# Gates' exponentials moved into the attention layers, silu's table loaded ahead of the tanh, and first chunks ahead of the routing

## What is computed

```python
x = x + _L0_attn_ref(_L0_cond_ref(x, side, side, w, u, cond), ...)
x = x + _L0_ffn_ref(_L0_cond2_ref(x, side, side, w, u, cond), ...)
...
# a gate: two scans over time (forward and back) of exp(k) and exp(k) * v, and then
euk = jnp.exp(jnp.minimum(u + kf, 30.0))
num = nf + nb - ekv + euk * vf
den = df + db - ek + euk
base = jax.nn.sigmoid(r) * (num / jnp.maximum(den, 1e-08))
...
# L0's feed-forward part: 16 experts, of which 6 are taken, and a shared one
scores = jax.nn.softmax(x @ gate_w.T, axis=-1)
topk_w, topk_ids = lax.top_k(scores, TOP_K)
y = jax.nn.silu(g) * u @ w2_.T
```

## Time and profile before

| | us |
|---|---|
| median of the three timed runs | 1056.41 |
| lowest, highest | 1053.12, 1060.1 |
| the profiled execution | 1053.54 |
| its span | 1051.7 |
| busy: TensorE, VectorE, ScalarE, GpSimd | 917.2, 787.1, 522.7, 248.9 |
| mean granted clock of TensorE, of full speed | 0.961 |

### The profile page before, as it was taken

One profiled execution on the slowest core, in us unless ns is written; L12 is line 12 of the kernel. 1 busy time (PEld: TensorE's weight loads), 2 busy tenths in 40 slices (PEclk: granted clock), 3 DMA queues, 4 the chain that ended last, 5 costly groups with the idle time before them and its releaser, 6 DMA issues.

```text
span 1051.7 us, 14774 instructions
## 1 busy us (share of the span) xinstructions
PE 917.2 (87%) x5524; PEld 672.9 (64%) x5524; DVE 787.1 (75%) x1188; ACT 522.7 (50%) x781; POOL 248.9 (24%) x288
## 2 busy tenths in 40 slices
PE   2899898899999998799888989996768886899998
PEld 1566666677777886556555868862445664778886
DVE  7898893459999895867967689887759998554444
ACT  6354446345545554355466444435857666243332
POOL 5122213023334241000020022301623224012221
PEclk9999998899999999879989999997999999899999
DMA  6000000243434330000000243324010000033331
GB/s 248 1 2 2 1 2 1 100 141 87 146 113 145 119 114 31 1 1 1 1 1 1 71 119 117 91 77 104 1 60 1 1 1 4 29 112 111 114 106 60
DMA packets 28518, 64.07 MB, mean 61 GB/s; under 512 B 10240, under 2 KB 12032, under 8 KB 27680
## 3 DMA queue, kind: packets, MB, share of 16 engines
q1 hardware_dynamic: 28448, 63.14, 18.9%
HBM read 60.37 MB, written 2.76 MB: 60 GB/s over the span
## 4 chain that ended last, share of the span: by engine, by line
PE 57%; DVE 22%; ACT 11%; issue 7%; POOL 1%; DMA 1%; DVEq 0%; SPq 0%; ACTq 0%; POOLq 0%
PE bank L1723 10%; PE bank L1724 10%; PE bank L1725 10%; PE bank L639 4%; PE bank L665 3%; DVE act_lo L2073 2%; ACT probs L786 2%; DVE wkv_y L192 2%; DVE bank L2068 2%; PE bank L748 1%; DVE bank L2059 1%; PE bank L2294 1%; DVE wkv_y L269 1%; PE bank L697 1%; DVE act_s L912 1%
## 5 line engine op out<-in xcount | busy, mean ns | idle before, releaser
L1723 PE MATMUL bank<-h_hi,w_gu_hi 128*128 128x512 f32 x416 | 168.1, 404 | 14.3 <-DVE act_lo L2073 11.1
L1870 ACT ACTIVATE act_s<-bank 128x512 f32<-128x512 f32 x104 | 61.8, 597 | 219.1 <-PE bank L1725 219.1
L1725 PE MATMUL bank<-h_lo,w_gu_hi 128*128 128x512 f32 x416 | 165.8, 399 | 0.0
L1724 PE MATMUL bank<-h_hi,w_gu_lo 128*128 128x512 f32 x416 | 165.7, 398 | 0.0
L2059 DVE TENSOR_TENSOR bank<-bank,c_rows 128x512 f32<-128x512 f32 x94 | 65.1, 692 | 87.9 <-PE bank L1725 87.9
L1990 POOL TENSOR_TENSOR w_d_lo<-w_raw,w_d_hi 128x256 fp32r<-128x256 f32 x52 | 46.9, 901 | 268.6 <-ACT w_d_hi L1864 268.6
L1723 PEld LDWEIGHTS bank<-h_hi,w_gu_hi 128*128 128x128 f32 x416 | 79.2, 190 | 41.3 <-issue 20.0
L786 ACT ACTIVATE probs<-bank 128x1536 f32<-128x1536 f32 (+1 forms) x32 | 53.0, 1657 | 99.0 <-PE bank L697 90.6
L1725 PEld LDWEIGHTS bank<-h_lo,w_gu_hi 128*128 128x128 f32 x416 | 78.9, 190 | 19.3
L1985 POOL TENSOR_TENSOR w_gu_lo<-w_raw,w_gu_hi 128x512 fp32r<-128x512 f32 x52 | 71.5, 1374 | 83.2 <-ACT w_gu_hi L1859 83.2
L1724 PEld LDWEIGHTS bank<-h_hi,w_gu_lo 128*128 128x128 f32 x416 | 79.2, 190 | 17.4
(11 more groups left out here) (345 smaller groups left out, 1808.9 us busy)
## 6 DMA issues: line engine op xcount, KB each, us to landing
w_raw<-in_L_w SPq DMA_DIRECT2D x52, 384.0 KB, 3.2
c_rows<-c_L SPq DMA_DIRECT2D x26, 512.0 KB, 3.6
c_rows<-c_L SPq DMA_DIRECT2D x6, 448.0 KB, 3.6
w_attn<-in_L_w_attn SPq DMA_DIRECT2D x2, 1280.0 KB, 7.5
c_rows<-c_L SPq DMA_DIRECT2D x6, 384.0 KB, 3.5
c_rows<-c_L SPq DMA_DIRECT2D x6, 320.0 KB, 3.6
c_rows<-c_L SPq DMA_DIRECT2D x6, 256.0 KB, 3.8
lora_chunks<-w_raw SPq DMA_DIRECT2D x4, 384.0 KB, 2.6
```

Of the source, the lines that this page charges most:

```text
L1723: pe.matmul(o, w_hi, r_hi, start=start, stop=False)
L1724: pe.matmul(o, w_lo, r_hi, start=False, stop=False)
L1725: return pe.matmul(o, w_hi, r_lo, start=False, stop=stop)
L1870: act.activation(act_s[:, half, :], bank[2 * half][:, :], ACT.Silu).then_inc(self.silu, 1)
```

## The change

It does four things.
- The exponentials of gates 2 and 3 (16) leave `Experts.act` of L0 for the last batch of L0's attention, in four groups of four (`gate_exps_act`); the 8 of gate 6 leave L1's experts for the end of L1's attention.
- Ahead of the first tanh of L0's and L1's experts the set of tables with silu is loaded by an own instruction.
- In L0, gate and up of chunk 1 for the first half stand ahead of the logits of the second half, the silu, product and split of chunk 0 for the first half stand in the attention's end, and the routing's exponential stands behind the high parts of the chunks. In L1 the silu and the product of the first half go ahead of the routing. `made` gives the new count of the steps of chunks 0 and 1 in L0.
- Steps of the routing that don't need the one ahead of them no longer wait for it (`note`), and in L3 some are exchanged.

```diff
+        def gate_exps_act(act, n, batches):
+
+            for b in batches:
+                for ch in range(KC):
+                    last = side_exp_act(act, G[:, G_SLOT[n], ch, b * T:b * T + T], ch, n, b)
+            if batches[-1] == B - 1:
+                last.then_inc(wkv_exp, B)
...
@@ -1041,14 +1049,23 @@
                     if b:
                         self.ctx_act(act, b - 1, 1)
                     self.exp_act(act, b, 0)
+                    if b == B - 1:
+                        gate_exps_act(act, 2, (0, 1))
                     if b == 0:
                         act.wait_ge(n_gated, self.first + 1)
                     self.inv_act(act, b, 0)
                     self.exp_act(act, b, 1)
+                    if b == B - 1:
+                        gate_exps_act(act, 2, (2, 3))
                     self.exp_act(act, b, 2)
+                    if b == B - 1:
+                        act.wait_ge(n_gated, B)
+                        gate_exps_act(act, 3, (0, 1))
                     self.scale_act(act, b, 1, 0)
                     self.scale_act(act, b, 1, 1)
                     self.ctx_act(act, b, 0)
+                    if b == B - 1:
+                        gate_exps_act(act, 3, (2, 3))
                     self.units_exp_act(act, b, 1)
                     self.inv_act(act, b, 1)
                 self.exp_act(act, B - 1, 3)
...
@@ -1110,6 +1127,8 @@
                 self.inv_dve(dve, B - 1)
                 self.norm_dve(dve, B - 1, 0)
                 self.norm_dve(dve, B - 1, 1)
+                F0.mul_dve(dve, 0, 0)
+                F0.lo_dve(dve, 0, 0)
                 self.tail_dve(dve, B - 1)
...
                 self.ctx_act(act, B - 1, 1)
+                act.wait_ge(n_proj, 4 * (self.first + B))
+                act.wait_ge(n_vproj, self.first + B)
+                gate_exps_act(act, 6, range(B))
                 F1.tanh_act(act, 0)
...
+            def made(self, p, half):
+
+                return 2 * half + p + 1 if self.plain and p < 2 else self.count(p, half)
...
                 if p:
-                    pe.wait_ge(L.silu if p == 2 and not L.plain else L.mul, L.count(p - 1, half))
+                    pe.wait_ge(L.silu if p == 2 and not L.plain else L.mul, L.made(p - 1, half))
                 else:
...
                 if L.name != "L0":
                     L.logits_pe(pe, 0)
                 if L.name == "L0":
+                    L.gate_up_pe(pe, 1, 0)
                     L.logits_pe(pe, 1)
                 else:
                     L.gate_up_pe(pe, 0, 0)
                     L.logits_pe(pe, 1)
                 L.gate_up_pe(pe, 0, 1)
                 if L.plain:
-                    L.gate_up_pe(pe, 1, 0)
                     L.down_pe(pe, 0, 0)
                     L.gate_up_pe(pe, 1, 1)
                     L.down_pe(pe, 0, 1)
...
             def silu_act(self, act, p, half):
-                act.wait_ge(self.gate_mm, self.count(p, half))
+                act.wait_ge(self.gate_mm, self.made(p, half))
                 if p:
-                    act.wait_ge(self.mul, self.count(p - 1, half))
+                    act.wait_ge(self.mul, self.made(p - 1, half))
                 act.activation(act_s[:, half, :], bank[2 * half][:, :], ACT.Silu).then_inc(self.silu, 1)
...
                 if half == 0:
+                    if L.name != "L3":
+                        act.preload_act_table_set("silu_and_others")
                     act.wait_ge(L.x_ready, L.x_value - B // 2)
                     if L.name == "L0":
                         act.wait_ge(n_tab, 11)
...
-                for unit in L.units[::B]:
-
-                    g = UNITS[unit][0]
-                    if g == 3:
-                        act.wait_ge(n_gated, B)
-                    if g == 6:
-                        act.wait_ge(n_gated, 2 * B)
-                    for b in range(B):
-                        for ch in range(KC):
-                            last = side_exp_act(act, G[:, G_SLOT[g], ch, b * T:b * T + T], ch, g, b)
-                    last.then_inc(wkv_exp, B)
+                if L.plain:
+                    L.silu_act(act, 0, 0)
+                    L.hi_act(act, 0, 0)
                 L.tanh_act(act, 1)
+                if L.name == "L1":
+                    L.silu_act(act, 0, 0)
                 L.split_h_act(act, 1)
-                L.route_act(act)
-                L.silu_act(act, 0, 0)
+                if L.plain:
+                    L.silu_act(act, 1, 0)
+                else:
+                    L.route_act(act)
+                    if L.name == "L3":
+                        L.silu_act(act, 0, 0)
                 L.silu_act(act, 0, 1)
...
                 else:
-                    L.hi_act(act, 0, 0)
-                    L.silu_act(act, 1, 0)
                     L.split_gu_act(act, 2)
                     L.hi_act(act, 0, 1)
+                    L.hi_act(act, 1, 0)
+                    L.route_act(act)
                     L.silu_act(act, 1, 1)
-                    L.hi_act(act, 1, 0)
                     L.copies_act(act)
...
+                if L.name != "L3":
+                    L.mul_dve(dve, 1 if L.plain else 0, 0)
                 L.route0_dve(dve)
-                L.mul_dve(dve, 0, 0)
-                L.route1_dve(dve)
-                L.mul_dve(dve, 0, 1)
                 if L.plain:
-                    L.lo_dve(dve, 0, 0)
-                    L.mul_dve(dve, 1, 0)
+                    L.mul_dve(dve, 0, 1)
                     L.lo_dve(dve, 0, 1)
+                    L.lo_dve(dve, 1, 0)
+                    L.route1_dve(dve)
                     L.mul_dve(dve, 1, 1)
-                    L.lo_dve(dve, 1, 0)
                 else:
+                    L.mul_dve(dve, 0, 0 if L.name == "L3" else 1)
+                    L.route1_dve(dve)
+                    if L.name == "L3":
+                        L.mul_dve(dve, 0, 1)
                     L.route2_dve(dve)
...
-            def done(self, dve, ins):
+            def note(self, ins):
+
                 self.steps += 1
                 ins.then_inc(self.r_step, 1)
+
+            def done(self, dve, ins):
+
+                self.note(ins)
                 dve.wait_ge(self.r_step, self.steps)
...
-                    do(dve.tensor_tensor(tb(3), lg, L.kth(0), ALU.subtract))
-                    do(dve.tensor_tensor(tb(2), lg, L.kth(5), ALU.is_gt))
+                    L.note(dve.tensor_tensor(tb(3), lg, L.kth(0), ALU.subtract))
+                    L.note(dve.tensor_tensor(tb(2), lg, L.kth(5), ALU.is_gt))
                     do(dve.tensor_tensor(tb(4), lg, L.kth(5), ALU.is_equal))
-                    do(dve.tensor_reduce(route_s[:, 0, :], tb(2), AX.X, ALU.add))
+                    L.note(dve.tensor_reduce(route_s[:, 0, :], tb(2), AX.X, ALU.add))
...
                     do(dve.tensor_scalar(tb(2), tb(2), 0.5, 0.5, ALU.mult, ALU.add))
+                    L.note(dve.tensor_scalar(tb(4), tb(2), -1.0, center, ALU.mult, ALU.add))
                     do(dve.tensor_scalar(tb(3), tb(2), lower, None, ALU.is_ge))
+                    L.note(dve.scalar_tensor_tensor(out=tb(4), in0=tb(2), scalar=center, in1=tb(4), op0=ALU.subtract, op1=ALU.max))
                     do(dve.scalar_tensor_tensor(out=tb(3), in0=tb(2), scalar=0.5, in1=tb(3), op0=ALU.is_le, op1=ALU.mult))
-                    do(dve.tensor_scalar(tb(4), tb(2), -1.0, center, ALU.mult, ALU.add))
-                    do(dve.scalar_tensor_tensor(out=tb(4), in0=tb(2), scalar=center, in1=tb(4), op0=ALU.subtract, op1=ALU.max))
                     dve.wait_ge(L.r_act, 2)
...
+                    L.note(dve.tensor_tensor(tb(4), tb(4), tb(3), ALU.mult))
                     L.largest_dve(dve, tb(5))
+                    L.note(dve.tensor_reduce(route_s[:, 0, :], tb(4), AX.X, ALU.add))
```

More of the change, by code:

```diff
@@ L1739, in up_pe @@
                 if p:
-                    pe.wait_ge(L.mul, L.count(p - 1, half))
+                    pe.wait_ge(L.mul, L.made(p - 1, half))
                 if p > (0 if L.plain else 1):
@@ L1873, in hi_act @@
                 if p or self.plain:
-                    act.wait_ge(self.mul, self.count(p, half))
+                    act.wait_ge(self.mul, self.made(p, half))
                 else:
@@ L2055, in weigh_dve @@
                 if p:
-                    dve.wait_ge(L.up_mm, L.count(p, half))
+                    dve.wait_ge(L.up_mm, L.made(p, half))
                 else:
-                    dve.wait_ge(L.mul, L.count(p, half))
+                    dve.wait_ge(L.mul, L.made(p, half))
                 dve.tensor_tensor(m, m, weights, ALU.mult).then_inc(L.weighted, 1)
@@ L2063, in mul_dve @@
                 if p == 0 or p < L.plain:
-                    dve.wait_ge(L.up_mm, L.count(p, half))
+                    dve.wait_ge(L.up_mm, L.made(p, half))
                 else:
                     dve.wait_ge(L.weighted, L.weights(p, half))
-                dve.wait_ge(L.silu, L.count(p, half))
+                dve.wait_ge(L.silu, L.made(p, half))
```

18 lines of the change are left out of this document (8 added, 10 removed).

## The result

The median of 20 runs is 1050.21 us (1047.56 to 1057.36) against 1056.76 us (1050.76 to 1069.41) of 20 runs of the kernel before; the ratio is 0.9946 with a 95% interval from 0.9924 to 0.9969. The forecast was 1050.5.

The account below looks back on a forecast made before the run. TensorE was taken as the bound, busy 917.2 of 1051.7 us, so only its waits and 1.2 GHz stretches could be won. Terms +1.0 − 5.4 + 0.0 − 0.2 = −4.6 from 1055.0 gave 1050.5 us, range 1045.5 to 1057.

Parts of the forecast that it names:

- Part 1: Last batch of L0's attention: sixteen exponentials moved in cost +1.0 us (0.6 by the first group, 0.4 by the fourth).
- a sign of being wrong: The forecast is wrong if L0's last attention batch is over 2 us longer, or its entry distance over 20.
- Part 2: L0's entry: chunk 1 ahead of the logits gains 5.4 us, chunk 2 starting at 205.3 instead of 210.68; bounds −5.6 to −3.3.
- I take 2.4 GHz throughout: L0's entry: TensorE keeps its full clock despite the small gaps, as between 573 and 578.
- the clock stays low: Rival, L0's entry: small gaps add up and the 1.2 GHz stretch stays; gain only 3.3 us, time 1052.5; chance 0.15.
- Those of 0.75 and 0.35: L0's entry: TensorE waits 0.75 us for product (0,1), then 0.35 for the routing's second part before turning the weights.
- Part 3: L1's entry: eight exponentials ahead of the first tanh, 4 us in ScalarE's wait, change 0; bounds −0.4 to +0.4.
- ends this piece: L1's entry: the weights' DMA, for which VectorE waits 4.00 us at 610.67, is issued at about the same time.
- Part 4: L3's entry: two routing waits fewer before the exponential, 0.1 each, gain 0.2 us; bounds −0.6 and 0.
- The dearer table switch: Rival, L0's entry: table loads cost more than their 1.28 us rows, gain 1.4 us less, time 1051.8; chance 0.10.
- The stall of 8 us: Rival, L0's attention: every exponential group delays TensorE, up to +8.0 us, making it 2.4 slower, 1057.4; chance 0.10.
- hidden: Rival, each entry: unmoved transfers or weights set its end; added 1.0 us, gain up to 1, time 1055.0; chance 0.07.

Follow-up runs that it names:

- exps_only: Kernel before with only the exponentials moved (L0's sixteen into its attention's last batch, L1's eight ahead of its first tanh); median 1062.17 us beside 1062.46 of before.
- after_again: The changed kernel run again with no edit, for a second profile; median 1052.28 us beside 1062.46 of the kernel before, ratio 0.9915.
- notes_late: Changed kernel with every routing wait back and, in L0, the split of chunk 2's gate and up weights moved behind silu (1,1); median 1053.81 us.
- two_loads: Changed kernel with two more activation table loads between the routing's exponential and silu (1,1) of L0; median 1054.5 us.
- notes_undone: Changed kernel with a wait behind every routing operation again; median 1052.92 us.
- l0_only: Kernel before with only L0's new order; exponentials, routing waits, L1 and L3 as before; median 1050.48 us beside 1058.29 of before, ratio 0.9926.
- split8_l3: Changed kernel with eight of L0's sixteen exponentials back in its experts, and L3's entry ordered like L1's; median 1050.73 us.

## Why the prediction was right, and where it was not

**Part 1, forecast +1.0.** +0.89 (B of exps_only, after_again and notes_late): 0.60 at the wait of 158.54 and 0.3 at the last score exponential, by the two steps named. What the step left out is the clock: of the seven traces with all groups four have 1.2 GHz in this batch, at 1.6 to 3.3 us. In all four the batch is over 2 us longer than before, which the prediction had named as a sign of being wrong: it took the sum of the waits for the batch's length and had no term for the clock there.

**Part 2, forecast −5.4.** In D −5.1 to −5.3. But in seven of the eleven traces with the new entry C is 16.0 instead of 15.0, although only 3.4 us of it are at 1.2 GHz and not 6.8. Before, the 1.2 GHz lies where TensorE has waits (at full clock it is busy 2.58 of 5.60 us there, 172.1 to 177.7 of after_again); the 3.4 us come behind that, on matmuls without a gap (busy 3.40 of 3.40). C and D together are 40.7 before, 36.2 to 36.7 in ten of the eleven, and 35.6 in the first trace of the changed kernel: some −4.2, and −5.1 in that one. The step that failed is "I take 2.4 GHz throughout". In eight of eleven traces with the new order 3.4 us of D run at 1.2 GHz; the rival "the clock stays low" was half right, with 1.2 of its 2.1 us (the terms written beside it give 2.0). The gaps of 0.45 and 0.6 came as 0.53 and 0.46. Those of 0.75 and 0.35 vanished where TensorE ran slow, and were 0.39 and 0.10 where it didn't (two_loads), so that the distance at full clock is an estimated 17.6 us instead of 17.9.

**Part 3, forecast 0.** F1 is 0.69 shorter, outside the bound of −0.4: the 0.50 wait went, and the 0.1 and 0.4 that I charged against it delayed nothing. But the weights come from DRAM when they came before, 16.5 to 17.1 us behind the start of F1 in all fourteen traces, and TensorE meets them just behind F1. Its wait there, in before and in after_again:

```profile
612.90 0.47 PE L1723 MATMUL bank<-act_hi,w_d_hi 128*128 128x512 f32 x1 [0.29 <-DVE act_lo L2073]
```

```profile
609.08 0.47 PE L1749 MATMUL bank<-act_hi,w_d_hi 128*128 128x512 f32 x1 [0.94 <-DVE act_lo L2098]
```

The piece from 612.21 to 700.39 took 87.6 to 88.2 us in the four traces with the old L1 and 88.0 to 88.8 in the ten with the new, means 87.9 and 88.4: most of the gain is given back, as "ends this piece" says.

**Part 4, forecast −0.2.** −0.28 with 3.4 us at 1.2 GHz on both sides, and notes_undone takes it back. In the two traces without, 18.88 (l0_only, L3 as before) and 18.35 (after_again), it is 0.53.

**The rivals.** The dearer table switch is refuted by rows: 1.29 from a load's start to the next instruction. The stall of 8 us is refuted: +0.89 for four groups, none for two. The gain was not hidden.

**The sum.** The rows of the changed places give +0.9 − 4.2 − 0.2 − 0.3 = −3.8, where the forecast was −4.6; the part that is off is part 2, at −4.2 instead of −5.4. The runs at equal clock give −3.9 ± 0.6, but that is not a check of the same quantity: the rows hold the clock's gain in C and D, where 6.8 us less run at 1.2 GHz in most traces (0.003 of the mean clock), and the difference at equal clock takes it out. The clock is higher wherever the new entry stands undisturbed: five kernels with it have mean clocks of 0.958 to 0.959, the two with the old one 0.952 and 0.955, though the three with waits or loads put back have 0.953 to 0.958. Of the 6.4 us between the mean spans the rows of the changed places explain 3.8; the other 2.6 would have to lie in code that wasn't changed, where the clock differs from run to run, and five traces of the two kernels don't show why they favour the changed one. That stays open.

**The time.** That 1050.5 met 1050.21 was partly luck. The medians of the two kernels lie 6.5 apart, 1.9 more than the 4.6 forecast, and the forecast started from 1055.0, 1.8 under the 1056.76 of 20 runs. The two misses cancelled. The 1.9 is itself made of a sum 0.8 too large and of the gain outside the changed places, which was not forecast.

## What to carry to other kernels

Compare two traces by stretches between the same instructions, with the us at the lower clock beside each; then a change of 0.3 us shows although runs scatter by 7. Work put into an engine's idle time costs nothing in the gap itself and its full excess ahead of something awaited: of four equal groups the two in gaps cost 0, the two ahead of the logarithm and the last scores 0.89. Where an engine's order lets it work through a wait of the others, as L0's chunk 1 does, expect part of the time at the lower clock to go too, and the rest to move: here it fell on full matmuls in C, and behind F3 in split8_l3. So compare a stretch together with its neighbours.

## What the hardware showed that I had not expected

A VectorE operation with both inputs in SBUF that started while GpSimd ran an operation on two SBUF inputs was held until GpSimd was done. In L0 of notes_undone it was 1.24 us instead of 0.29 (above); l0_only has the same 1.24. In L3 of after_again:

```profile
909.00 1.29 POOL L2010 TENSOR_TENSOR w_gu_lo<-w_raw,w_gu_hi 128x512 fp32r<-128x512 f32 x1 [17.91 <-ACT w_gu_hi L1885]
909.01 0.19 DVE L2276 RECIPROCAL route_s<-route_s 128x8 f32<-128x8 f32 x1
...
909.24 1.14 DVE L2277 TENSOR_TENSOR probs<-probs,route_s 128x64 f32<-128x64 f32 x1
910.29 0.15 DVE L2278 TENSOR_TENSOR route_s<-route_s 128x8 f32<-128x8 f32 x1
```

The reciprocal, with one input, is not held; the product behind it ends at 910.38, GpSimd at 910.29. One input isn't always enough to escape. In split8_l3 a TENSOR_SCALAR that started 0.10 into GpSimd's operation took 1.22 us, the next one of its size 0.16:

```profile
910.74 1.29 POOL L2005 TENSOR_TENSOR w_gu_lo<-w_raw,w_gu_hi 128x512 fp32r<-128x512 f32 x1 [16.41 <-ACT w_gu_hi L1880]
910.84 1.22 DVE L2254 TENSOR_SCALAR route_s<-route_s 128x8 f32<-128x8 f32 x1
911.98 0.16 DVE L2255 TENSOR_SCALAR route_s<-route_s 128x8 f32<-128x8 f32 x1
```

The Trainium skill, "SBUF — State Buffer", section "SBUF: two separate sides", says that the two engines share a pair of ports as an exclusive lock, which a VectorE operation takes when it has two SBUF inputs and GpSimd's reads SBUF, or when it runs in a two-port mode. The traces agree for two inputs, with the 1.24 and 1.14 us above; in which mode the TENSOR_SCALAR ran, no trace here shows. The changed kernel misses this collision in L0 by about 0.1 us at full clock: in two_loads GpSimd starts at 202.22 (its row is 1.32 long), 0.1 behind the start of the routing's last operation.

Operations of VectorE on 128x128 start 0.20 apart when none waits, though each row is 0.29 long, and 0.33 apart with a wait. And L1's attention, in code that wasn't touched, takes about 167 us with 31 us at 1.2 GHz in it, or 172 with 44 to 51.
